# A scatter of edge records with at most four indirect DMAs in flight

## The chip, the cores and the metric

The kernel runs on one core of one Trainium2 chip. The metric is the device time of one execution in microseconds (us). Three timed runs of the kernel before gave 2790.8, 2792.78 and 2793.15 us, so the median is 2792.78 us. The profile beside them is that of one more execution. The engines are named as in the profile: PE (TensorE matmul), PEld (its weight load), DVE (VectorE), ACT (ScalarE), POOL (GpSimd) and SP (SyncE, which only issues DMAs here).

## The reference

The inputs are 1250 nodes with 512 features (`x`), 40000 edges (`src`, `dst`), 128 features and one weight per edge, and the parameters of four graph layers. The reference runs four layers one after the other: a mean over neighbours added to a dense product (layer 0), two rounds of edge attention with eight heads and a feed-forward part (layer 1), a weighted sum over edges (layer 2), and messages made of edge features and source rows, followed by two multilayer parts with norms (layer 3). In each of them the sum over edges goes to the node `dst`. In short:

```
sums  = segment_sum(beta[dst], src); out0 = x @ wc + sums / counts + bias      # layer 0
scores = einsum(q[tgt], k[srcidx]); softmax over the edges of tgt; segment_sum  # layer 1, twice
segment_sum(edge_weight * (x @ W)[src], dst)                                    # layer 2
segment_sum(relu(x[src] + edge_attr @ W_edge), dst), then two MLPs with norms   # layer 3
```

All layers use the same edges. The kernel therefore first sorts the edges once, and all stages after that read the sorted lists.

## The kernel before, in words

The 40000 edges lie in the input as 125 partitions with 320 columns each (`EC`). The first block of the program, `sort_edges`, gives each edge a slot in a sorted list, grouped by the block of 128 nodes that holds `dst` and by the third of the nodes that holds `src`. An edge's record has four numbers (source, place of the destination, weight, number of the edge) and stands in the tile `rec`; the number of its slot stands in `pos3`. DVE makes `pos3` by scans over 30 classes and sums, then signals `pos_ready` (line 392).

The records are brought to their slots in two ways, at the same time:

- Columns 0 to 159 (`PE_COLS`) go by TensorE. For each column DVE and ACT build one-hot matrices (lines 401 to 406 and 592), and PE multiplies five of them into PSUM banks (line 550), where the sums of all 160 columns gather. The last signal of PE lets ACT copy one bank (line 596), and DVE adds it (line 477).
- Columns 160 to 319 go by POOL. For each column `scatter_edges` issues one indirect DMA (line 196), which writes 128 records of four floats from SBUF to the slots in DRAM (`slots3_dram`) that `pos3` names. Each DMA adds 16 to one of two semaphores, `scattered[0]` or `scattered[1]`, when it has landed. In the kernel before, the two take turns every eight columns, and before the columns 16, 24, 32 and so on POOL waits until the eight columns before last have landed.

SP has its own list: it loads the inputs, then fills the two large accumulators with zeros (line 289, 1.28 MB and 6.4 MB), then waits for both `scattered` semaphores at their full count (line 292), and reads the whole list of slots back from DRAM (line 293, 864 KB). DVE waits for this read (line 478) and adds the part that TensorE made (line 480). Everything after this needs the sum: PE turns it (line 561), ACT copies it, PE moves the tiles to their final places (line 567), and DVE splits the weights (lines 481 to 493). The block ends with a barrier of all engines. The next block, `edge_matrices`, starts with DVE line 633, and a loop over 108 groups of edges follows. No instruction of a later block starts ahead of that barrier.

Of the kernel before, what the change touches and what calls it, by code (L numbers as in the profile page):

```python
# [23 lines left out]
EC = 320  # L24
# [109 lines left out]
def row_of(vector):  # L134

    return vector.rearrange("(o n) -> o n", o=1).to_broadcast([P, vector.shape[0]])
# [42 lines left out]
PE_COLS = 160  # L179
PARTS = 5  # L180
SHOTS, UPDATE = 9, 4

def updates_to(column):
# [4 lines left out]
def scatter_edges(pool, first, edge_pos, rec, slots_dram, slots, scattered):  # L189

    for n, c in enumerate(range(first, EC)):
        i, u = n // 16, n // 8 % 2
        if n % 8 == 0 and i:
            pool.wait_ge(scattered[u], 128 * i)
        pool.indirect_dma_start(  # L196
            out=slots_dram, out_offset=bass.IndirectOffsetOnAxis(ap=edge_pos[:, c:c + 1], axis=0),
            in_=rec[:, c, :], in_offset=None, bounds_check=slots - 1, oob_is_err=False).then_inc(scattered[u], 16)

def sort_edges(nc, k, a):
# [6 lines left out]
    scattered, read_back = [S(f"scattered3{u}") for u in range(2)], S("read_back3")  # L208
# [55 lines left out]
    with nc.Block() as block:  # L264
        T, OFF, TOT, GRP, GS, M = range(6)

        @block.sync
        def _(sp):

            sp.wait_ge(cleared, 4)  # L270
            sp.dma_start(dst_i[0:EP, :], a.dst.rearrange("(p c) -> p c", c=EC)).then_inc(loaded, 16)
            sp.dma_start(src_i[0:EP, :], a.src.rearrange("(p c) -> p c", c=EC)).then_inc(loaded, 16)
            sp.dma_start(ew_s[0:EP, :], a.edge_weight.rearrange("(p c) -> p c", c=EC)).then_inc(loaded, 16)

            whole = (N // P) * P
            sp.dma_start(k.alpha[:, 0:N // P, :], a.x[0:whole, :].rearrange("(b p) f -> p b f", p=P)).then_inc(x_loaded, 16)
            sp.dma_start(k.alpha[0:N - whole, N // P, :], a.x[whole:N, :]).then_inc(x_loaded, 16)
            sp.dma_start(wn[:], a.L0_gnn_wn.rearrange("(c p) n -> p c n", p=P)).then_inc(wn_loaded, 16)
            sp.dma_start(wc[:], a.L0_gnn_wc.rearrange("(c p) n -> p c n", p=P)).then_inc(wc_loaded, 16)
            sp.wait_ge(pads_made, 1)  # L280
            sp.dma_start(k.slots3_dram.rearrange("(p t) w -> p (t w)", p=P),
                         pads[:].rearrange("p t w -> p (t w)")).then_inc(prefilled, 16)
            sp.dma_start(bias[:], row_of(a.L0_gnn_bias)).then_inc(bias_loaded, 16)

            sp.wait_ge(zeros_made, 1)
            sp.wait_ge(alpha_added, NB)
            for acc, first, end in ((acc_c, ACC_BY_ACT, NB * NP // 512), (acc_a, 0, NB * NP // 512)):
                sp.dma_start(acc[:, first:end, :], zeros[:].unsqueeze(1).to_broadcast([P, end - first, 512])).then_inc(zeroed, 16)

            for u in range(2):
                sp.wait_ge(scattered[u], 16 * len([n for n in range(EC - PE_COLS) if n // 8 % 2 == u]))
            sp.dma_start(slots[:].rearrange("p t w -> p (t w)"),
                         k.slots3_dram.rearrange("(p t) w -> p (t w)", p=P)).then_inc(read_back, 16)
            sp.wait_ge(zeroed, 32)
            sp.wait_ge(read_back, 16)

        @block.gpsimd
        def _(pool):
            constants(pool, k, made)  # L300
            pool.iota(k.rec[:, :, 3], pattern=[[1, EC]], base=0, channel_multiplier=0,
                      allow_small_or_imprecise_dtypes=True).then_inc(id_made, 1)
            pool.wait_ge(id_made, 1)
            pool.wait_ge(columns_made, 1)
            pool.tensor_scalar(k.rec[:, :, 3], k.rec[:, :, 3], id_col[:, 1:2], None, ALU.add).then_inc(id_made, 1)
            pool.wait_ge(w_high_made, 1)
            pool.tensor_tensor(ew_low[:], ew_s[:], ew_high[:].bitcast(F32), ALU.subtract).then_inc(w_low_made, 1)
            pool.wait_ge(id_made, 2)
            pool.wait_ge(rec_copied, 2)
            pool.wait_ge(pos_ready, 1)  # L310
            pool.wait_ge(prefilled, 16)
            scatter_edges(pool, PE_COLS, pos3, k.rec, k.slots3_dram, P * NT3, scattered)
            for u in range(2):
                pool.wait_ge(scattered[u], 16 * len([n for n in range(EC - PE_COLS) if n // 8 % 2 == u]))

        @block.vector
        def _(dve):
# [2233 lines left out]
```

## Time and profile before

| What | Value |
|---|---|
| median of three runs | 2792.78 us |
| profiled execution, span from first to last instruction | 2795.5 us |
| PE busy | 2528.3 us, 90% |
| DVE busy | 2138.1 us, 76% |
| ACT busy | 1682.1 us, 60% |
| POOL busy | 1299.1 us, 46% |
| scatter by POOL, first to last issue | 66.5 to 283.9 us |
| DMA queues | 338.46 MB, mean 121 GB/s |

The profiled execution has no time beside its span in the page, so the span of 2795.5 us stands for it; it lies 2.7 us above the median of the timed runs. The span is divided into 40 slices of 69.9 us; the sort of the edges is in the first five of them. A digit in a row of slices is the busy share in tenths. In a row of the timeline stand the start (us), the duration (us), the engine, the line, the operation, the tiles, and, in brackets, how long the engine was idle before it and what ended that.

### The profile page before, as it was taken

To read this page: it belongs to the slowest core of one execution; us is meant where nothing else is said; L and a number is where in the kernel's file an instruction comes from. 1 tells how busy PE (TensorE), PEld (TensorE's weight loads), DVE (VectorE), ACT (ScalarE), POOL (GpSimd) and SP (SyncE) were. 2 spreads that over 40 slices of the span, in tenths; PEclk is the share of its full clock that TensorE was granted. 3 is DMA by queue.
4 is the path that set the end of the run, shared out by engine and by line. 5 is a ranking of instruction groups with operands and counts; after the bars stand their busy time and mean duration, and the time that the engine had idled before them with its cause. 6 is when DMAs were issued, how large, how long until landed. Compare 5 with 4: busy or idle time off the path is not lost. (4 is left out here: it accounts for less than half of the span.)

```text
span 2795.5 us, 45377 instructions
## 1 busy us (share of the span) xinstructions
PE 2528.3 (90%) x13039; PEld 1993.9 (71%) x13039; DVE 2138.1 (76%) x4172; ACT 1682.1 (60%) x3746; POOL 1299.1 (46%) x1279
## 2 busy tenths in 40 slices
PE   6999899999799999879899989598999999987887
PEld 4598555554488999648799984366888888765766
DVE  9699899998537888553588874866999999866667
ACT  1299888872226777413477761324888888845560
POOL 1777000007305677640377667315777777710211
PEclk9999999999899999998999999899999999988999
DMA  2210000013344453324455447225888888840201
GB/s 90 78 40 3 13 0 0 0 43 123 124 179 121 145 147 112 124 76 158 112 149 140 146 107 91 98 89 188 276 276 278 274 273 278 232 104 32 78 1 45
DMA packets 126768, 338.46 MB, mean 121 GB/s; under 512 B 25255, under 2 KB 39530, under 8 KB 126638
## 3 DMA queue, kind: packets, MB, share of 16 engines
q0 software_dynamic: 60768, 172.88, 22.0%
q1 hardware_dynamic: 65870, 163.93, 18.0%
q8 instruction: 71, 1.16, 0.2%
q14 instruction: 59, 0.48, 0.1%
HBM read 243.04 MB, written 85.82 MB: 118 GB/s over the span
## 5 line engine op out<-in xcount | busy, mean ns | idle before, releaser
L1839 POOL DMA_INDIRECT x_got<-table_dram,src_idx x376 | 418.8, 1114 | 117.3 <-issue 99.3
L722 POOL DMA_INDIRECT feature_rows<-in_edge_attr,ids x376 | 367.4, 977 | 117.4 <-issue 110.1
L1969 DVE TENSOR_TENSOR msg<-bank,x_got 128x512 f32<-128x512 f32 x376 | 252.7, 683 | 73.6 <-PE bank L1864 53.5
L1278 DVE TENSOR_TENSOR pt_low<-bank,pt_high 128x640 fp32r<-128x640 f32 x320 | 262.8, 822 | 54.9 <-ACT pt_high L1241 53.4
L673 ACT ACTIVATE hot_rest<-hot_dst,slot_w 128x128 bf16<-128x128 bf16 x864 | 272.6, 399 | 38.4 <-DVE hot_dst L633 38.4
L1241 ACT CAST pt_high<-bank 128x640 fp32r<-128x640 f32 x320 | 219.9, 688 | 117.6 <-PE bank L1192 117.4
L725 POOL COPY ids<-id_idx 128x136 uint32<-128x136 uint32 (+2 forms) x5 | 1.2, 242 | 612.5 <-DVE id_idx L840 347.6
L1918 ACT ACTIVATE msg_high<-msg 128x512 fp32r<-128x512 f32 x329 | 206.8, 628 | 74.8 <-DVE msg L1969 74.8
L1272 DVE CUSTOM_DVE_ANT_0 p<-bank,log_counts 128x1254 f32<-128x1254 f32 x160 | 232.6, 1454 | 13.7 <-PE bank L1175 13.6
L1192 PE MATMUL bank<-ident,p 128*128 128x128 f32 x1600 | 229.1, 275 | 2.3 <-DVE pt_low L1278 2.3
L1949 DVE SCALAR_TENSOR_TENSOR msg_low<-msg,msg_high 128x512 fp32r<-128x512 f32 x329 | 223.7, 680 | 0.0
L1233 ACT ACTIVATE p<-p,bound 128x1254 f32<-128x1254 f32 x160 | 215.7, 1348 | 8.3 <-DVE bound L1272 8.3
L196 POOL DMA_INDIRECT slots_dram<-rec,pos x160 | 168.5, 1053 | 103.7 <-issue 103.4
L1203 PE MATMUL bank<-pt_high,val 128*128 128x256 f32 x800 | 213.3, 301 | 0.9 <-DVE agg_t L1284 0.9
L1204 PE MATMUL bank<-pt_low,val 128*128 128x256 f32 x800 | 199.8, 285 | 0.0
L1192 PEld LDWEIGHTS bank<-ident,p 128*128 128x128 f32 x1600 | 190.9, 142 | 11.8 <-issue 3.2
L1174 PE MATMUL bank<-keys,queries 128*128 128x418 f32 x480 | 187.0, 390 | 11.5 <-DVE bound L1272 7.2
L1175 PE MATMUL bank<-keys,queries_low 128*128 128x418 f32 x480 | 174.0, 362 | 0.0
L694 PE MATMUL bank<-hot_src,hot_rest 128*128 128x417 bf16 x864 | 171.3, 340 | 0.0
L550 PE MATMUL bank<-row_hot,col_part 125*128 125x432 f32 x800 | 164.2, 366 | 6.1 <-ACT col_part L592 5.3
L550 PEld LDWEIGHTS bank<-row_hot,col_part 125*128 125x128 f32 x800 | 147.1, 190 | 23.6 <-DVE row_hot L406 13.3
L1877 PE MATMUL bank<-msg_high,hot_t 128*128 128x512 f32 x329 | 149.4, 454 | 11.6 <-DVE msg_low L1949 11.5
(408 smaller groups left out, 6687.9 us busy)
## 6 DMA issues: line engine op xcount, KB each, us to landing
features_dram<-feature_parts POOLq DMA_DIRECT2D x94, 512.0 KB, 3.0
edge_got<-features_dram SPq DMA_DIRECT2D x94, 512.0 KB, 4.9
qk_dram<-qk_high SPq DMA_DIRECT2D x16, 640.0 KB, 2.9
qk_dram<-qk_low SPq DMA_DIRECT2D x16, 640.0 KB, 4.2
keys<-qk_dram SPq DMA_DIRECT2D x32, 320.0 KB, 4.7
queries<-qk_dram SPq DMA_DIRECT2D x32, 320.0 KB, 6.7
queries_low<-qk_dram SPq DMA_DIRECT2D x32, 320.0 KB, 8.9
acc_a<-zeros SPq DMA_DIRECT2D x1, 6400.0 KB, 30.6
```

Of the source, the lines that this page charges most:

```text
L550: m = pe.matmul(ps_p[:, q, :], col_part[0:EP, u, q, :], row_hot[0:EP, u, :], start=(c == 0), stop=(c == PE_COLS - 1))
L673: last = act.activation(hot_rest[:, u, j, q, :], hot_dst[:, u, :, j], ACT.Copy, scale=k.slot_w[:, 1 + q, bass.ds(g * GT + j, 1)])
L722: pool.indirect_dma_start(out=rows[:, g % 2, j * ED:(j + 1) * ED], out_offset=None, in_=self.a.edge_attr_128, in_offset=bass.IndirectOffse ...
L1192: t = pe.transpose(unit(i)[:, j * P:(j + 1) * P], p[:, n % AHEAD, (u * HALF + j) * P:(u * HALF + j + 1) * P], k.ident[:])
L1203: pe.matmul(to, v, p_high[:, slot, j, :], start=(u == 0 and j == 0), stop=False)
L1233: act.activation(rows, rows, ACT.Exp, bias=bound[:, n % 4:n % 4 + 1], scale=-1.0, accum_out=sums[:, n // (2 * NB) % 2, n % NB, n // NB % 2 ...
L1241: act.copy(p_high[:, made % 3, :, n % 2 * P:(n % 2 + 1) * P], unit(2 * n + u).rearrange("p (j n) -> p j n", n=P)).then_inc(high_made, 1)
L1272: dve.tensor_tensor_reduce(out=thirds(p[:, n % AHEAD, :]), in0=k.bank[:, 0:3, 0:THIRD], in1=thirds(k.log_counts[:, n % NB, :]), scale=-1.0 ...
L1278: dve.tensor_tensor(p_low[:, made % 3, :, columns], unit(2 * n + u).rearrange("p (j n) -> p j n", n=P), p_high[:, made % 3, :, columns].bi ...
L1839: pool.indirect_dma_start(out=xg[:, g % XRING, j, :], out_offset=None, in_=k.table_dram, in_offset=bass.IndirectOffsetOnAxis(ap=k.src_idx[ ...
L1949: dve.scalar_tensor_tensor(low[:, u, j, :], msg[:, j, :], 0.0, high[:, u, j, :].bitcast(F32), ALU.max, ALU.subtract).then_inc(low_done, 1)
L1969: dve.tensor_tensor(msg[:, j, :], k.bank[:, 2 + j, :], xg[:, r, j, :], ALU.add).then_inc(added_x, 1)
```

## The change

A new constant `REST = 4` takes the place of the eight in the turns of the two semaphores. POOL now waits before each column whose number is a multiple of four (but the first), and it waits on the other semaphore, the one of the four columns just issued, at a count that all of these have landed. The counts for which SP and POOL wait at the end are adapted; their sums are the same. The number of DMAs, what they write, and the programs of all other engines stay the same.

```
+REST = 4
...
-        i, u = n // 16, n // 8 % 2
-        if n % 8 == 0 and i:
-            pool.wait_ge(scattered[u], 128 * i)
+        q, u = n // REST, n // REST % 2
+        if n % REST == 0 and n:
+            pool.wait_ge(scattered[1 - u], 16 * REST * ((q + 1) // 2))
         pool.indirect_dma_start(
...
-                sp.wait_ge(scattered[u], 16 * len([n for n in range(EC - PE_COLS) if n // 8 % 2 == u]))
+                sp.wait_ge(scattered[u], 16 * len([n for n in range(EC - PE_COLS) if n // REST % 2 == u]))
...
-                pool.wait_ge(scattered[u], 16 * len([n for n in range(EC - PE_COLS) if n // 8 % 2 == u]))
+                pool.wait_ge(scattered[u], 16 * len([n for n in range(EC - PE_COLS) if n // REST % 2 == u]))
```

This is the list of POOL in the block `sort_edges` before the change, from its last computation on; a row with x15 stands for 15 instructions, and `scattered30` and `scattered31` are the semaphores `scattered[0]` and `scattered[1]`:

```order
L307 TENSOR_TENSOR ew_low<-ew_s,ew_high 128x320 [waits ew_high_made]
L196 DMA slots_dram<-rec,pos_88 55296x4 [waits pos_ready,slots_prefilled,rec_copied,id_made]
L196 DMA slots_dram<-rec,pos_88 55296x4 x15
L196 DMA slots_dram<-rec,pos_88 55296x4 [waits scattered30]
L196 DMA slots_dram<-rec,pos_88 55296x4 x7
L196 DMA slots_dram<-rec,pos_88 55296x4 [waits scattered31]
```

The last two kinds of rows go on in turns: 18 waits in all, each for eight columns that were issued eight columns earlier. This is the same place of POOL's list after the change (the diff adds a line, so line 196 is 197):

```order
L308 TENSOR_TENSOR ew_low<-ew_s,ew_high 128x320 [waits ew_high_made]
L197 DMA slots_dram<-rec,pos_88 55296x4 [waits pos_ready,slots_prefilled,rec_copied,id_made]
L197 DMA slots_dram<-rec,pos_88 55296x4 x3
L197 DMA slots_dram<-rec,pos_88 55296x4 [waits scattered30]
L197 DMA slots_dram<-rec,pos_88 55296x4 x3
L197 DMA slots_dram<-rec,pos_88 55296x4 [waits scattered31]
```

The DMAs stand in the same order; only the waits have moved. There are 39 of them now, and each is for the four columns directly ahead of it.

## Rows read from the trace of the kernel before

**Rows 1.** The page: the span, busy slices of three engines, POOL's scatter.

```profile
span 2795.5 us, 45377 instructions
...
PE   6999899999799999879899989598999999987887
...
DVE  9699899998537888553588874866999999866667
...
POOL 1777000007305677640377667315777777710211
...
L196 POOL DMA_INDIRECT slots_dram<-rec,pos x160 | 168.5, 1053 | 103.7 <-issue 103.4
```

**Rows 2.** What the engines waited for: SP to 420 us, then POOL.

```profile
SPq L292 <- DMA slots_dram<-rec,pos: 164.8, 1, 164.8
...
POOL slots_dram L196 <- DMA slots_dram<-rec,pos: 0.3, 1, 0.3
...
POOL feature_rows L722 <- POOL ids L725: 4.2, 5, 0.9
```

**Rows 3.** The timeline at the end of the scatter and after it.

```profile
283.87 0.98 POOL L196 DMA_INDIRECT slots_dram<-rec,pos  x1 [0.30 <-issue]
...
286.03 0.33 SPq L293 DMA_DIRECT2D slots<-slots_dram  x1
...
288.69 0.52 ACT L596 COPY pe_w<-bank 128x432 f32<-128x432 f32 x1 [1.61 <-PEq L555]
...
289.31 0.61 DVE L477 TENSOR_TENSOR pe_w<-bank,pe_w 128x432 f32<-128x432 f32 x1 [6.10 <-ACT pe_w L596]
...
290.59 0.94 DVE L480 TENSOR_TENSOR slots<-bank,slots 128x432 f32<-128x432 f32 x1 [0.67 <-DMA slots<-slots_dram]
...
302.12 0.43 DVE L633 TENSOR_TENSOR hot_dst<-row_of_each,slot_dst 128x512 bf16<-128x512 f16 x1 [0.40 <-PEq L264]
```

**Rows 4.** The timeline at the start of the scatter.

```profile
64.99 0.49 DVE L392 TENSOR_TENSOR pos<-lin,oob 128x320 uint32<-128x320 f32 x1
...
66.55 1.50 POOL L196 DMA_INDIRECT slots_dram<-rec,pos  x1 [53.90 <-issue]
68.35 1.21 POOL L196 DMA_INDIRECT slots_dram<-rec,pos  x1 [0.30 <-issue]
69.86 0.98 POOL L196 DMA_INDIRECT slots_dram<-rec,pos  x1 [0.30 <-issue]
```

**Rows 5.** Line 196 in 160:286: durations, issue to landing; last, landings in 130:142.

```profile
L196 POOL DMA_INDIRECT slots_dram<-rec,pos x92: 977/992/1417, 159.4 to 283.9; - x92
...
DMA to landing us min/median/max: 2.1/2.1/3.5
...
DMA to landing us min/median/max: 8.3/8.6/8.9
```

**Rows 6.** The two zero fills; busy tenths of the DMA engines in 118:158.

```profile
119.78 0.73 SPq L289 DMA_DIRECT2D acc_c<-zeros  x1
120.55 0.64 SPq L289 DMA_DIRECT2D acc_a<-zeros  x1
...
DMA  0008999999999999999999999999999400000000
...
acc_a<-zeros SPq DMA_DIRECT2D x1, 6400.0 KB, 30.6
```

**Rows 7.** Another indirect DMA of POOL, after a wait at rest.

```profile
632.40 0.21 POOL L725 COPY ids<-id_idx 128x40 uint32<-128x40 uint32 x1 [347.56 <-DVE id_idx L840]
633.52 1.02 POOL L722 DMA_INDIRECT feature_rows<-in_edge_attr,ids  x1 [0.90 <-POOL ids L725]
634.84 0.96 POOL L722 DMA_INDIRECT feature_rows<-in_edge_attr,ids  x1 [0.30 <-issue]
```

**Rows 8.** Stretches: PE, PEld, DVE, ACT, POOL busy; granted clock; DMA share, GB/s.

```profile
304.00:308.00 4.00, 4.00 (x12) 1.78 (x13) 2.06 (x7) 3.59 (x12) 0.00 (x0) 0.50 0.00 0
308.00:312.00 4.00, 4.00 (x23) 2.32 (x22) 2.77 (x9) 1.81 (x6) 0.00 (x0) 0.99 0.00 0
```

## The prediction

> **What bounds the kernel now.** I read the page first. PE is 90% busy over the whole span, but the change touches one block in the first tenth of it, so the averages say little. The digits of POOL are 7 through slices 2 to 4, and the costliest group of POOL there is the scatter of line 196: 160 indirect DMAs, 1053 ns each, and between them a steady idle time put down to "issue" [rows 1]. So I asked which wait ends last at the end of that block. The waits of SP show one of 164.8 us at line 292 for the scatter to land [rows 2]: SP has nothing else to do, and the read-back behind it starts when the scatter ends. The timeline there is the view that decides. The last column is issued at 283.87, SP starts the read-back at 286.03, and DVE starts to add at 290.59, released by that read. The other half of the sort, by PE, is done at nearly the same time: DVE adds PE's fourth bank from 289.31 to 289.92 and then waits only 0.67 us [rows 3]. The two halves are balanced, and POOL's half is already the later one by 0.67 us. All that follows (turning, moving, splitting, the barrier, and the first instruction of the next block at 302.12) hangs on the add at 290.59. So each microsecond by which the scatter ends later moves the rest of the program by one.
>
> Is the scatter bound by POOL or by its waits? In the trace there is one wait of a column for a landing, 0.3 us long, the same as the gap between any two columns [rows 2]. In the steady part a column takes 0.98 us of issue and a gap of 0.30, that is 1.28, and from 159.4 to 283.9 the mean step is 124.5 / 91 = 1.37 [rows 4, 5]. Landing takes 2.1 us from issue [rows 5], and as the waits of before look back eight columns (some 10 us), they never hold the engine.
>
> **The change part by part.** The DMAs, their number and their order stay. The 18 waits that held nothing go, and that saves nothing. In come 39 waits, each for the four columns directly ahead. The last of these lands 2.1 us after its start; without the wait the next column would start 1.28 us after it. So the landing alone exposes 2.1 - 1.28 = 0.82 us.
>
> To this comes the restart, the time from the signal to the first issue. No row of this line shows it for a landing. Two rows are near: DVE ends `pos` at 65.48 and the first column starts at 66.55, 1.07 us later [rows 4]; the feature gather restarts after a signal of its own engine with 0.90 us once, 4.2 / 5 = 0.84 in the mean [rows 2, 7]. I take 0.95, in the middle. The lower bound is nothing, if the next column is prepared while POOL waits. The upper one is 1.07 and an issue that is slow after rest: the first column took 1.50 instead of 0.98, 0.52 more [rows 4], though the gather's first took only 1.02 [rows 7]. So a wait costs 0.82 + 0.95 = 1.77 us, between 0.82 and 2.41. Over 39 waits this is 69 us, between 32 and 94.
>
> Behind the waiting POOL stand only its own later columns and, behind the block's end, nothing before the gather at 632. Who waits for them is SP's read-back, and through it DVE, PE and ACT.
>
> The zero fills come in between. SP starts them at 119.78 and 120.55, the DMA engines are nine tenths busy until about 150, and columns issued then land after 8.3 to 8.9 us [rows 5, 6]. Before, this was hidden by the eight columns of distance. The fills start when DVE has added `alpha`, which doesn't hang on POOL, so they stay where they are. A group of four takes 3 x 1.28 + 2.1 + 0.95 = 6.9 us when undisturbed. The groups then begin at about 67.3 + 6.9 k: number 7 issues its last column at 119.4, just ahead of the fill, number 8 at 126.3 and number 9 at 139.8; number 10 does so at about 153, after it. Two groups pay 8.6 - 2.1 = 6.5 more: 13 us. By the phase it can be one or three, so 6.5 to 19.5.
>
> A rule of the Trainium skill bears on this (DMA: Bandwidth & Descriptors, Queues, rings and completion order): each DMA engine takes turns between the queues at whole packets. By it a small DMA waits for the other queue's packets however few columns are in flight, and the 8.6 stays. If the 8.6 was instead a backlog of the 8.6 / 1.31, some 6.6 columns that were in flight, four would land in about 5.3, the fill would cost 6 and the sum below would be 7 less.
>
> Back the other way: the mean step of 1.37 lies 0.09 over the bare 1.28, and the surplus appears as issues of up to 1.42 us [rows 5]. After 288.7 PE, DVE and ACT have no more work in the block. If the surplus is due to them, the some 46 columns that will be issued after that save 46 x 0.09 = 4 us; at worst nothing.
>
> The Trainium skill has a rule for this as well (SBUF — State Buffer, Who interferes with whom): VectorE in its two-port modes and GpSimd lock each other out of a shared pair of ports. By it the longer issues vanish when DVE rests, and the 4 us are right; if they had another cause, the sum would be 4 higher.
>
> PE will rest some 80 us instead of a few before the turns at line 561, and the granted clock will be low for them. After the short rest of before it was already 0.50 in 304:308 and 0.99 in the stretch behind it [rows 8]. So little can be lost on top: 0 to 2 us, I take 1.
>
> Sum: 69 + 13 - 4 + 1 = 79 us. Against the profiled execution, 2795.5 + 79 = 2874.5; the timed median lies 2.7 under that span, so 2871.8, or 2872. With all lower ends, 32 + 6.5 - 4 = 34.5 and 2827; with all upper ends, 94 + 19.5 + 2 = 115.5 and 2908.
>
> **The rivals.**
>
> *Only the landing is exposed.* POOL's sequencer or the descriptor code prepares the next column during the wait, so the restart is nothing. For it: in the undisturbed scatter all gaps are 0.30 however the sequencer's own waits fall. Against it: both restarts from rest in the trace show 0.84 to 1.07. Time: 32 + 13 - 4 + 1 = 42, 2835.
>
> *Each restart is slow.* The first column after every wait takes 1.50, as the very first did, and three groups meet the fill. For it: the second and fourth columns were long too, 1.21 and some others 1.4. Against it: the gather's first took 1.02 [rows 7]. Time: 94 + 13 + 1 = 108 up to 115, 2900 to 2908.
>
> *Nothing changes.* The change doesn't do what it says, because the four have landed when POOL comes to the wait. It would need a landing within 1.28 us of the issue; the fastest shown is 2.1 [rows 5]. Time: 2793.
>
> *Not slower, by a lighter queue.* With at most four columns in flight each is issued without its surplus. All surplus is 168.5 us less 160 x 0.977, that is 12.2 us [rows 1, 5]. This decides only if a wait costs under 12.2 / 39 = 0.31 us, while the landing alone costs 0.82. And the gain would be cut off at 0.67 us, where DVE comes to wait for PE's half instead [rows 3]. Time: 2792.
>
> **How the numbers follow.** My forecast, drains of landing plus restart, gets 0.78, and its own range is 2858 to 2898 (restart 0.84 with one group in the fill, up to 1.07 with half of the slow firsts and three groups). Only the landing: 0.09. Slow restarts: 0.10. No change: 0.02. Not slower by a lighter queue: 0.01, and it lies within what is no change. The range from 2846 to 2904 holds the forecast and about half of the slow restarts, and leaves out the other end. A measurement of this kernel tells about 0.2%, or 5.6 us, from no change. So slower by more has 0.97, within it 0.025, and faster 0.005.
>
> **What would show it.** In the profile after, the scatter should end at about 363 instead of 284; each fourth gap should be about 2.07 us (2.1 - 0.98 + 0.95) instead of 0.30 and put down to the DMA of the scatter; two or three gaps in 120:151 should be near 8.6. The wait of SP at line 292 (then 293) should be about 244 us, and DVE should wait some 78 us for the read-back. The sort's other half should still end near 289, and the span from the add at line 480 to the end should stay at 2505 us. I am wrong if the gaps are near 1.1 (no restart), if the first column of each group takes 1.5, or if a later stage gets shorter or longer by several microseconds.

## The result, and the profile after

On the chip of the traces above the changed kernel takes 2865.49 us (median of four runs, 2856.7 to 2867.94), the kernel before 2792.97 (four runs with the first three among them). The ratio is 1.0248, with a 95% interval from 1.0227 to 1.0269: slower by 72.5 us, where 79 were forecast. In the experiments a second kind of chip turned up on which the sign is the other way; that is told from the first experiment on, and it is the larger lesson of this case.

The page of the kernel after, the span and the rows that answer to [rows 1]; after that its waits (engine, line, tile, what it waited for: us in all, times, longest), which answer to [rows 2]:

```profile
span 2862.1 us, 45377 instructions
...
PE   6999089999978999978999998598999999987887
...
DVE  9698089999743888845378885556999999866667
...
POOL 1555500001710776761067676414777777720221
```

```profile
SPq L293 <- DMA slots_dram<-rec,pos: 237.2, 1, 237.2
...
POOL slots_dram L197 <- DMA slots_dram<-rec,pos: 89.2, 39, 9.6
```

POOL's digits have gone from 7 to 5 and reach one slice further, and in that slice PE and DVE stand at 0. POOL now waits 39 times for a landing, 89.2 us in all, where [rows 2] had one wait of 0.3. SP's wait is 72 us longer, and DVE waits 73.7 us for the read-back (its row stands below) instead of 0.67 [rows 3].

The timeline of POOL in the kernel after, an undisturbed group and the two that met the zero fills:

```profile
80.31 1.06 POOL L197 DMA_INDIRECT slots_dram<-rec,pos  x1 [1.88 <-DMA slots_dram<-rec,pos]
...
84.24 0.98 POOL L197 DMA_INDIRECT slots_dram<-rec,pos  x1 [0.30 <-issue]
87.10 0.98 POOL L197 DMA_INDIRECT slots_dram<-rec,pos  x1 [1.88 <-DMA slots_dram<-rec,pos]
...
125.48 0.98 POOL L197 DMA_INDIRECT slots_dram<-rec,pos  x1 [0.30 <-issue]
134.51 0.98 POOL L197 DMA_INDIRECT slots_dram<-rec,pos  x1 [8.05 <-DMA slots_dram<-rec,pos]
...
149.50 1.24 POOL L197 DMA_INDIRECT slots_dram<-rec,pos  x1 [9.58 <-DMA slots_dram<-rec,pos]
```

Each fourth gap is about 1.88 us. With the issue of 0.98 that is 2.86 from the start of the last column; landing takes 2.1 of it, so the restart (from the landing to the next issue) is 0.75 us. Two gaps, not three, are as long as 8 us.

The end of the scatter in the timeline of the kernel after, which answers to [rows 3]:

```profile
355.48 0.98 POOL L197 DMA_INDIRECT slots_dram<-rec,pos  x1 [0.30 <-issue]
357.64 0.33 SPq L294 DMA_DIRECT2D slots<-slots_dram  x1
362.10 2.61 DVE L481 TENSOR_TENSOR slots<-bank,slots 128x432 f32<-128x432 f32 x3 [73.73 <-DMA slots<-slots_dram]
...
373.63 0.42 DVE L634 TENSOR_TENSOR hot_dst<-row_of_each,slot_dst 128x512 bf16<-128x512 f16 x1 [0.40 <-PEq L265]
```

The last column is issued 71.6 us later than before, the add starts 71.5 later, and so does the next block (373.63 against 302.12). From there on this one execution is 4.9 us shorter than the one of before (2488.5 against 2493.4), which the medians of the timed runs don't show: they differ by 72.5. The same stretch takes from 2490.6 to 2496.2 us in the four traces from chip 11 (experiments 9 to 12), so it differs by several microseconds without this change as well.

### The profile page after: what moved, and what is told of

The parts are those of the page before. It is cut to its first block and busy times, and to the rows that moved or that the text cites. A ratio compares the mean times of both kernels' runs of the same rounds, so it can differ in the third digit from the quotient of the medians.

```text
span 2862.1 us, 45377 instructions
## 1 busy us (share of the span) xinstructions
PE 2532.1 (88%) x13039; PEld 1997.5 (70%) x13039; DVE 2132.2 (74%) x4172; ACT 1683.3 (59%) x3746; POOL 1292.7 (45%) x1279
## 5 line engine op out<-in xcount | busy, mean ns | idle before, releaser
L1919 ACT ACTIVATE msg_high<-msg 128x512 fp32r<-128x512 f32 x329 | 206.8, 629 | 72.4 <-DVE msg L1970 72.2
L197 POOL DMA_INDIRECT slots_dram<-rec,pos x160 | 163.0, 1019 | 181.6 <-issue 92.5
L1863 PE MATMUL bank<-w_edge_high,edge_turned 128*128 128x512 f32 x376 | 155.3, 413 | 2.8 <-DVE msg L1970 2.8
```

## The experiments

Where times of the whole program and ratios are compared below, both kernels ran on the same chip. The start of the next block (the first row of the tile `hot_dst` on DVE) is given for each, since it measures the sort by itself; in the kernel before it is at 302.1, on the first chip, and starts from traces of other chips are compared with that. "Chips of the first kind" are the one of the traces above and chip 11, on which the kernel before takes 2791 to 2793 us. On chips 5 and 15 it takes 3060 and 3045 us; these are "of the second kind". Each numbered chip was visited once. The runs therefore show two kinds of behaviour, each steady through the executions of the kernel before on one visit (17 on chip 5, 7 on chip 15, 13 on chip 11); whether this belongs to the chip for good or to something else that was fixed during the visit isn't shown.

**1. The changed kernel again.** No edit. It ran on chip 5.

> The changed kernel once more, to have its interval and a second trace. The theory is that each of 39 full drains exposes the landing of its last column and a restart of POOL (2.1 + 0.75 - 1.28 = 1.57 us each, 61 in all), the zero fill adds 14, and a calmer issue gives back 4 or so. It expects the last column to be issued 71 to 73 us later than in the kernel before, and the time 71 to 73 us longer as well. The rival, that something behind the sort gets shorter (the first two traces differ by 66.6 us in all but by 71.5 at the start of the next block), expects 66 to 68 us and the same 5 us missing at the same place.

Measured on chip 5: 2963.91 us against 3059.89 for the kernel before, a ratio of 0.9679 (0.9661 to 0.9697). Neither theory stands: the change makes the program 96 us faster here. Yet the sort is as on the first chip, the last column is issued at 354.6 and the next block starts at 372.8 (373.6 there). So it isn't the changed sort that differs between the chips, and what is left is the sort of before and later stages.

**2. Waits that look back.** `REST` stays 4, and each wait is for the group before the last.

```
-        if n % REST == 0 and n:
-            pool.wait_ge(scattered[1 - u], 16 * REST * ((q + 1) // 2))
+        if n % REST == 0 and q >= 2:
+            pool.wait_ge(scattered[u], 16 * REST * (q // 2))
```

> 38 waits, one every four columns as in the changed kernel, but each for the four columns before the last four (4 to 8 in flight). The theory (what costs is the drained queue, not the wait) expects gaps of 0.30 us everywhere outside the zero fill, inside it a group every 6.6 us instead of 5.2, and 3 to 9 us in all over the kernel before. The rival (each wait stops POOL's sequencer and costs its restart, whatever it waits for) expects 25 to 60 us.

Measured on chip 5: 3061.18 us, a ratio of 0.9998 (0.9988 to 1.0009). POOL has the same number of waits as experiment 1 within one and none of its gaps, so the waits themselves cost POOL nothing; the drains do, or, on this chip, gain. What the expectation says of the time inside the zero fill wasn't tested, as the fills start only at 291.11 here, behind the last column. As its time is that of the kernel before, I take its trace to show what happens there. These are rows of the kernel with waits that look back, the stretch 120:240 (columns as in [rows 8]), then its waits, then a piece of its timeline:

```profile
120.00:240.00 120.00, 32.34 (x32) 8.89 (x31) 6.94 (x10) 0.00 (x0) 90.64 (x93) 0.50 0.03 2
...
DVE alpha L434 <- remote: 182.6, 9, 21.0
...
106.77 1.01 PE L515 MATMUL bank<-wc,xt_in 128*128 128x512 f32 x1 [2.21 <-issue]
108.17 0.29 PEld L515 LDWEIGHTS bank<-wc,xt_in 128*128 128x128 f32 x1 [2.51 <-issue]
109.60 1.01 PE L515 MATMUL bank<-wc,xt_in 128*128 128x512 f32 x1 [1.82 <-issue]
...
206.95 1.01 PE L515 MATMUL bank<-wc,xt_in 128*128 128x512 f32 x1 [1.79 <-issue]
227.97 0.69 DVE L434 TENSOR_TENSOR alpha<-bank,alpha 128x512 f32<-128x512 f32 x1 [20.98 <-remote]
```

The same stretch in the kernel before on the first chip:

```profile
120.00:240.00 120.00, 114.69 (x561) 103.77 (x560) 115.16 (x424) 107.67 (x368) 91.99 (x88) 0.97 0.26 68
```

In these 120 us PE does 32 matmuls instead of 561 and DVE 10 instructions instead of 424, while POOL does its columns as ever (93 and 88). PE waits for nothing that the trace shows ("issue"): a weight load and a matmul start in turns, one instruction each 1.40 us. DVE is held up by itself too, and not only through PE: the matmul at 206.95 is the last of line 515, and yet DVE adds the banks that these matmuls filled at 227.97, 250.40, 272.80 and 289.60. Its waits are put down to "remote", which names no engine of the trace. The last column is issued early, at 274.2, but PE's half is then far behind: ACT copies PE's bank at 459.2 instead of 288.7, and the next block starts at 472.1 instead of 302.1. From 300 to 460, behind POOL's last column, PE does 766 matmuls. This starving of the other engines costs 170 us.

**3. One column left in flight.** Each fourth column counts on the second semaphore, and POOL waits for the first three of a group alone.

```
-        q, u = n // REST, n // REST % 2
+        q, u = n // REST, int(n % REST == REST - 1)
...
-            pool.wait_ge(scattered[1 - u], 16 * REST * ((q + 1) // 2))
+            pool.wait_ge(scattered[0], 16 * (REST - 1) * q)
```

> Every four columns POOL waits for the first three of the last four, so that one column may still be in flight. The theory, in which landing (2.1) and restart (0.75) start at the issue of the column waited for and run beside the last column's own issue, expects the next column 2.85 us after the third one instead of 2.56: 0.29 x 39 = 11 us, and 2 or 3 groups in the zero fill at 6.5, together 22 to 30 us. If the restart can begin only when POOL is at rest, the gap is 0.75 instead of 0.59 and it is 6 more. If the wait itself or a less than full queue is what costs, it stays near the 72 of the changed kernel.

Measured on chip 5: 3024.03 us, a ratio of 0.9885 (0.9861 to 0.9908). POOL does as the theory has it. A piece of its timeline with one left in flight:

```profile
81.95 0.98 POOL L197 DMA_INDIRECT slots_dram<-rec,pos  x1 [0.30 <-issue]
83.50 1.07 POOL L197 DMA_INDIRECT slots_dram<-rec,pos  x1 [0.58 <-issue]
```

The gap is 0.58 us (0.59 expected), and the last column is issued at 302.1, 18 us later than in the kernel before on the first chip (22 to 30 expected). The restart runs beside the issue of the column ahead. But the other engines are starved here too, to a lesser degree: PE does 82 matmuls in 120:240, and the next block starts at 429.7. As DVE comes late, so do the fills: they start near 214 instead of 120.

**4. The restart by itself.** To the kernel before this adds, every four columns, a memset and a wait for its signal; no landing is waited for.

```
+        if n % 4 == 0 and n:
+            pool.memset(tick[:], 0.0).then_inc(ticked, 1)
+            pool.wait_ge(ticked, n // 4)
```

> The kernel before with its own waits, and every four columns a memset of one element per partition on POOL, for whose signal POOL waits; no landing is waited for. It measures the restart by itself. If the 0.75 us between a landing and the next issue is POOL's own way from its sequencer to the engine, each of the 39 gaps is about 0.9 us (memset 0.1, signal and restart 0.8) instead of 0.30, and the time grows by 23 to 28 us, with nothing more in the zero fill. If the 0.75 belongs to the DMA queue that has run empty, the gaps are 0.3 to 0.45 and the time grows by less than 6.

Measured on chip 5: 2941.09 us, a ratio of 0.9597 (0.9571 to 0.9623). Two rows of its timeline:

```profile
84.11 0.12 POOL L197 MEMSET tick<- 128x1 f32 x1
85.01 1.00 POOL L199 DMA_INDIRECT slots_dram<-rec,pos  x1 [0.77 <-issue]
```

From signal to issue it is 0.77 us, with no DMA in the wait. So the 0.75 us behind a landing is POOL's own way, and doesn't belong to an empty queue. The last column comes 18.8 us later than in the kernel before on the first chip, where 23 to 28 us were expected in the time. The gain on this chip shows one thing more: a pause of 0.9 us without any landing frees most of the other engines. PE does 327 matmuls in 120:240, and the next block starts at 374.4, bound by PE's half (its bank is copied at 361.5), while the last column is issued at 302.7.

**5. A drain every eight columns** (`REST = 8`).

> A full drain every eight columns. 19 drains at 1.57 us are 30, two groups meet the zero fill for 13, a calmer issue gives back 2 or 3: 38 to 42 us over the kernel before, and gaps of 1.87 us as with four. A rival, that a drain costs more the more columns it drains, expects gaps well over 1.87 and above 50 us.

Measured on chip 15: 2921.73 us against 3044.52, 0.9586 (0.9555 to 0.9618). The usual gap is 1.87 us, the same for eight as for four. The next block starts at 343.5: 41.4 us after the 302.1 of an undisturbed sort, where 38 to 42 were expected. PE's half is nearly free (copied at 290.7). The expected time itself was for the first kind of chip and was not met.

**6. A drain every two columns** (`REST = 2`).

> A full drain every two columns. 79 drains at 1.57 us are 124, three groups meet the zero fill for 20, a calmer issue gives back 6 to 10: 132 to 142 us over the kernel before, the gaps still 1.87 us.

Measured on chip 15: 3021.51 us, 0.9915 (0.9889 to 0.9940). The usual gap is 1.87 again and the next block starts at 445.9, 143.8 over 302.1 (132 to 142 expected, so a little more). With experiments 1 and 5 the sort grows by 41, 71 and 144 us for 19, 39 and 79 drains.

**7. The zero fills behind the read-back.** The two lines that issue the fills on SP move from ahead of the wait for the scatter to behind the issue of the read-back.

> Drains every four columns as in the changed kernel, but SP issues the two zero fills behind the read-back of the slots instead of during the scatter. If the two gaps of 8.05 and 9.58 us are due to the fill, both are gone, and the last column is issued 14 us earlier, near 342 instead of 355.5. The fills of some 31 us are then open at the end of the block, so the next block starts 3 to 8 us later than with the changed kernel, and the time is 2868 to 2874. If the long gaps have another cause (they come at the change from one kind of work to another), they stay and the time grows by 18 or more.

Measured on chip 15: 2954.05 us, 0.9696 (0.9669 to 0.9722). The longest gap of POOL is 3.3 us instead of 9.6, the last column is issued at 342.7 (342 expected), and the next block starts at 376.2. That is 2.6 us later than in the changed kernel on the first chip and 3.4 later than on chip 5 (3 to 8 expected), though the add starts 11 us earlier: DVE waits for the block's barrier for 14.2 us, with the fills now open at the end. This gives the collision with the fill its size: 355.5 - 342.7 = 12.8 us against the first chip, 354.6 - 342.7 = 11.9 against experiment 1, which ran on the second kind as this one did.

**8. 184 columns for PE, 136 for POOL** (`PE_COLS = 184`, drains every four).

> Drains every four columns, but PE takes 184 columns and POOL 136. Six groups less at 6.7 us end POOL's half 40 us earlier; PE's half ends 24 x 1.03 = 25 us later, near 314, and so is still the earlier one (the read-back lands near 322). The time falls by 40 us against the changed kernel, to 2825. If PE's half was what set the end, the time would grow by 25 instead.

Measured on chip 15: 2914.92 us, 0.9564 (0.9540 to 0.9588). The last column is issued at 317.5, PE's bank is copied at 312.1, and the next block starts at 335.7, 37.9 us earlier than in the changed kernel (40 expected). So POOL's half was what set the end.

**9. The kernel before again.** No edit. It ran on chip 11, of the first kind, as did the three that follow.

> The kernel before, unchanged, for a trace on one of the chips on which it takes 3045 to 3060 us instead of 2793. If the reading of the kernel with waits that look back holds, PE's half of the sort is starved while POOL issues without a pause: last column issued near 274 to 285, but the next block starts near 470 instead of 302, and the time is about 3050. On a chip like the first one the next block starts at 302 and the time is 2793.

Measured: 2793.10 us (ten runs, 2784.01 to 2796.87). The last column is issued at 285.3 and the next block starts at 303.5, as in the first trace. The chip thus left the case of the second kind untested; no trace of the kernel before itself on such a chip exists.

**10. The own signal every eight columns** (`n % 8`, count `n // 8`).

> As the kernel with its own signal, but a pause only every eight columns: the gap is 0.9 us 19 times, so a column takes 1.36 us in the mean. Theory A (the other engines are starved when POOL's columns follow each other faster than about one in 1.4 us in the mean) expects the starving to return, with the next block at 400 to 450 and 2990 to 3030 us where the kernel before takes 3050. Theory B (any regular pause is enough) expects at most 375 and 2940. On a chip like the first one: 12 us over the kernel before.

Measured on chip 11: 2805.73 us against 2790.58, 1.0046 (1.0029 to 1.0062). That is 15 us, and the next block starts at 314.0, 10.5 after that of experiment 9 (12 expected). Between its two theories on the second kind it decides nothing.

**11. The own signal twice every four columns.** Memset and wait stand twice in a row.

> Two signals of its own every four columns, so gaps of about 1.8 us 39 times and a column each 1.65 us in the mean, with no landing waited for. Theory A expects no starving: PE's half ends near 290, the last column is issued near 330, the next block starts near 348 and the time is 2925 to 2940 where the kernel before takes 3050. A theory C, that it is the emptied queue of the changed kernel that frees the other engines, expects PE's half as late as with one signal (its bank copied at 361) or later, and 2940 or more. On a chip like the first one: 45 to 48 us over the kernel before.

Measured on chip 11: 2823.28 us, 1.0108 (1.0091 to 1.0124). That is 33 us, not 45 to 48, and the expectation was wrong. Two rows of its timeline:

```profile
202.11 0.28 POOL L198 MEMSET tick<- 128x1 f32 x2
203.17 0.97 POOL L200 DMA_INDIRECT slots_dram<-rec,pos  x1 [0.77 <-POOL tick L198]
```

The second memset starts right behind the first, although it stands behind a wait; only the indirect DMA needs 0.77 us. So the restart is a cost of issuing an indirect DMA after a wait, not of the wait; which part of the issue takes it is not shown. The time also says that pauses alone are a loss where nothing is starved.

**12. A drain every eight columns and 176 columns for PE.**

> A full drain every eight columns and 176 columns for PE, the version to which the runs so far point for chips of the second kind. POOL's 144 columns end near 302, PE's half near 305, so the next block starts near 320, 15 to 25 us earlier than with 184 columns for PE and a drain every four. The time is 2895 to 2910 where the kernel before takes 3050. On a chip like the first one it is 2810, 17 us over the kernel before.

Measured on chip 11: 2812.95 us, 1.0074 (1.0056 to 1.0092), so 22 us over the kernel before (17 expected). The next block starts at 318.3 (320 expected), as PE's half, copied at 304.2, and POOL's, last issued at 300.2, are near each other. On a chip of the first kind the kernel before stays the fastest of all that ran. On the second kind experiments 8, 5 and 4 are 4.4, 4.1 and 4.0% under the kernel before, with intervals that overlap, so no best one can be named; this version wasn't tried there.

## Why the prediction was right, and where it stops

**What bounds the block.** Right. The add waits for the read-back, 1:1: 71.6 us at the last column are 71.5 at the add and at the next block. Experiment 8 confirms it from the other side.

**The drain.** The mechanism was right, its size a bit too large. Forecast 1.77 us each, of which 0.95 restart; measured 1.88 - 0.30 = 1.58, with a restart of 0.75. Experiments 3 and 4 show both parts by themselves. Both rows that the 0.95 was taken from, 0.84 and 1.07, lay above what a restart of this line costs; why isn't shown. Over 39 drains this is 61.6 instead of 69, that is 7.4 less, and the forecast of 79 missed by 6.5: the errors of the other terms, told below, nearly cancel, which is luck. No first column of a group took 1.50; the 39 of them took 1.02 in the mean and 1.45 at most, the others 1.02 as well.

**The zero fill.** Forecast 13, two groups. The two long gaps exceed 1.88 by 6.2 and 7.7, together 13.9; experiment 7 gives 11.9 to 12.8. A last landing there took 8.3 and 10.2 us with at most four columns in flight, so it was no backlog that four would shrink. The turns between queues that the Trainium skill states (DMA: Bandwidth & Descriptors, Queues, rings and completion order) fit this.

**The calmer issue.** Forecast 4 back. Line 196 was busy for 168.5 us; line 197 took 290.8 from first start to last end less 127.8 of gaps (92.5 - 53.9 + 89.2), that is 163.0. So 5.5 came back: 3.1 of it in the last 40 columns, behind 291, where the forecast had put all of it (for 46 columns), and the rest before. From 290 to 350, with DVE at rest, all 36 issues took 977 to 981 ns. This is as the lock of the Trainium skill has it (SBUF — State Buffer, Who interferes with whom), though no run took DVE's work away by itself. In experiment 2, where DVE, PE and ACT are all nearly at rest, the issues in 160:285 took 0.99 in the mean instead of 1.05.

**The clock of PE.** Forecast 1. The granted clock was 0.50 through the rest and the turns of PE, and its matmuls at line 568 took 3.51 us in all instead of 2.47 at line 567 of the kernel before. So PE did lose the 1 us, but the chain from the add to the next block is 11.53 us in both traces: the loss was hidden behind other work, and the term is nothing.

The sum of what was measured is 61.6 + 13.9 - 5.5 = 70.0, against 72.4 for the scatter from its first to its last issue (289.8 against 217.3). The rest are three single gaps of 2.81, 2.27 and 3.13 us between 267 and 291, 4.2 us over the usual ones, of which the kernel before had one (1.63 us, 1.3 over). Their cause is left open.

**The forecast's own signs.** The scatter ended at 355.5 (363 forecast), the gaps were 1.88 (2.07), SP waited 237.2 (244) and DVE 73.7 (78). One sign of being wrong did turn up: the span from the add to the end was 2500.0 us instead of 2505. The traces of chip 11 show such differences between executions too, and the timed medians don't have it.

**The rivals.** "Only the landing is exposed" fell to the restart of 0.75 us. The lower end that the forecast gave itself, 2858, doesn't follow from its terms: 39 x (0.82 + 0.84) + 6.5 - 4 is 67, hence 2860; nothing hangs on it. "Each restart is slow" fell with the firsts. "A lighter queue" was rejected for the first chip rightly. But its look at how many are in flight was closer to the point than I gave it: landing takes 2.1 us and a column 1.37, so in the kernel before some 1.5 columns are in flight outside the fill. "At most four" hardly limits anything there. What the change really adds is a pause of 1.6 us every four columns.

**Where it stops.** The 0.97 for "slower" was given for the kernel, but it holds for the chips of the first kind. On chip 5 the same change is 3.2% faster, so that the number came out right by where it was measured, and that part is luck. No row of the first trace showed it, since on that chip PE does its 561 matmuls in the stretch whatever POOL does. The cause as far as the runs show it: on the second kind, dense indirect DMAs of POOL hold up the instructions of PE, ACT and DVE. Outside the fill, the mean step from one column to the next and the time at which PE's bank was copied were:

| Experiment | Mean step | Bare step | PE's bank copied |
|---|---|---|---|
| 2, waits that look back | 1.31 us | 1.28 us | 459.2 us |
| 3, one left in flight | 1.38 us | 1.35 us | 416.9 us |
| 4, own signal | 1.49 us | 1.43 us | 361.5 us |
| 5, drain every eight | 1.60 us | 1.48 us | 290.7 us |
| 1, drain every four | 1.75 us | 1.68 us | 287.0 us |

The bare step is an estimate from the rows: 0.98 of issue and the usual gaps, such as (4 x 0.98 + 3 x 0.30 + 1.88) / 4 for experiment 1, without the longer issues and the stray gaps. It is the fairer column, since an issue is longer where the other engines work, and so the mean step is in part an effect of their being free. By either column the starving fades as the step grows, whether the pause comes from a drain or not. But the mean number of columns in flight (an estimate: 2.1 us of landing over the step) falls along with it, so this is an order and not a cause: that it is the mean step and not the length of the pauses was to be told apart by experiments 10 and 11, which ran on the first kind, and stays open. What is held up (the fetch of instructions, the signals, or a path to memory) was not settled; the instruction queues moved three packets in 66:160 of experiment 2 and three in 66:118 of the kernel before, so there was no flood of them. The step alone doesn't starve the engines: on the first kind it was 1.37 in the kernel before, and PE did its 561 matmuls.

The later stages of the second kind are slower as well. The gather of line 1840 lasts from 2007.7 to 2616.8, 609 us, against 1986.6 to 2517.6, 531 us, on the first chip. It took 603 to 610 us in all the traces from chips 5 and 15 and 530 to 532 in the others, whatever the sort did. That is most of the 100 us by which experiment 1 trails the changed kernel there.

## What to carry to other kernels

A wait for the landing of DMAs that were just issued costs the landing plus the way of the next issue, less the step that would have passed anyway: here 2.1 + 0.75 - 1.28 = 1.57 us, times the number of drains, and all of it counts if that engine's half is the later one. Ask how many are in flight before limiting them; here it was 1.5. And a trace shows one chip: when a change thins out what POOL issues beside PE and DVE, measure on several chips before calling it a loss or a gain, since here the same change took 2.5% more time on one kind and 3.2% less on the other.

## What was not expected of the hardware

- The kernel before differs by 9 to 10% between visits to different chips (2793 against 3045 and 3060 us). As far as traces show it, most of the difference sits where POOL issues indirect DMAs: 170 us in the sort (experiment 2, in place of the kernel before) and 78 in the gather of line 1840 (experiment 1).
- On the second kind PE may get one instruction each 1.40 us beside such a stream, and run nearly freely again with pauses in it (bank copied at 290.7 with a drain every eight columns).
- An indirect DMA behind a wait starts 0.75 to 0.77 us after the signal, whether it comes from a landing or from POOL itself, while a memset behind a wait starts at once. With one column still to be issued the 0.75 is hidden: the gap was 0.58.
- Beside a fill that keeps the DMA engines nine tenths busy, 128 records of 16 bytes land after 8.3 to 10.2 us instead of 2.1, also with at most four such DMAs in flight.
